# Identity products issued on TensorE ahead of its waits, in the attention block and the decay block of a four-layer network

## The reference

```
h = layernorm(x); q, k, v = h@wq+bq, h@wk+bk, h@wv+bv          # 64 wide
x = x + softmax(mask(q k^T / 8)) v @ wo + bo                   # causal, one head
h = layernorm(x); e = argmax(h@Wg + bg)                        # 1 of 8 experts
x = x + gelu(h@W1[e] + b1[e]) @ W2[e] + b2[e]
```

```
h = rmsnorm(x); mix tokens by decaying low-rank factors (h@u, h@v, length one)
and by a causal convolution of 4 taps, on h@proj_w; residual
h = rmsnorm(.); x = . + gelu(h@mlp_w1 + b1) @ mlp_w2 + b2
h = layernorm(x); x = x + gated linear map of the chosen expert (8 experts, capacity)
```

## Time and profile before

| what | value |
|---|---|
| median of 3 runs | 1574.55 us (1572.63 to 1575.88) |
| the profiled execution: its own time | 1564.02 us |
| its span from first to last instruction | 1562.3 us |
| mean granted TensorE clock | 0.891 |
| attention block (`c_`) in the trace | 1057.8 to 1324.8 us |
| decay block (`d_`) in the trace | 1324.8 us to the end |

### The profile page before, as it was taken

One profiled execution on the slowest core, in us unless ns is written; L12 is line 12 of the kernel. 1 busy time (PEld: TensorE's weight loads), 2 busy tenths in 40 slices (PEclk: granted clock), 3 DMA queues, 4 the chain that ended last, 5 costly groups with the idle time before them and its releaser, 6 DMA issues. The chain is left out here.

```text
span 1562.3 us, 21889 instructions
## 1 busy us (share of the span) xinstructions
PE 1274.7 (82%) x6731; PEld 720.4 (46%) x6731; DVE 1028.1 (66%) x2781; ACT 799.4 (51%) x1600; POOL 534.6 (34%) x668
## 2 busy tenths in 40 slices
PE   5899999999997128945589989985799997699898
PEld 1233333333332117941345655563476665477633
DVE  7878888888863665634897776323466654567486
ACT  2467777776774004526656653322445553466554
POOL 3442343343110005438555334431112112433046
PEclk7799999999999557975689999996799999699999
DMA  5211111111104402210023234221113131100001
GB/s 150 59 51 31 50 48 42 42 52 53 32 12 134 95 1 57 63 38 21 14 55 56 63 73 79 61 55 36 61 59 115 59 113 55 34 1 1 1 21 34
DMA packets 80775, 81.17 MB, mean 52 GB/s; under 512 B 19899, under 2 KB 64139, under 8 KB 80659
## 3 DMA queue, kind: packets, MB, share of 16 engines
q1 hardware_dynamic: 77327, 74.06, 18.2%
q0 software_dynamic: 2304, 4.72, 1.3%
q10 hardware_dynamic: 1028, 0.98, 0.2%
HBM read 64.32 MB, written 13.92 MB: 50 GB/s over the span
## 5 line engine op out<-in xcount | busy, mean ns | idle before, releaser
L933 DVE TENSOR_REDUCE a_nm<-a_aps 128x1 f32<-128x512 f32 x512 | 333.7, 687 | 74.7 <-PE a_aps L698 74.7
L897 ACT ACTIVATE a_prob<-a_sps 128x512 f32<-128x512 f32 x512 | 271.3, 597 | 114.6 <-PE a_sps L710 113.7
L698 PE MATMUL a_aps<-a_K,a_Q 96*128 96x512 bf16 x512 | 195.4, 402 | 12.5 <-DMA a_K<-k_parts 12.3
L710 PE MATMUL a_sps<-a_Q,a_K 99*128 99x512 bf16 x512 | 156.6, 386 | 1.2 <-ACT a_prob L897 1.2
L1402 POOL TENSOR_TENSOR p_h<-p_sl,p_t 128x512 f32<-128x512 f32 x72 | 105.5, 1483 | 144.6 <-issue 54.5
L719 PE MATMUL a_ops<-a_prob,a_Vg 128*32 128x512 f32 x1024 | 136.9, 609 | 0.0
L698 PEld LDWEIGHTS a_aps<-a_K,a_Q 96*128 96x128 bf16 x512 | 50.4, 98 | 139.9 <-DVE a_nm L933 89.8
L1542 ACT ACTIVATE p_sl<-p_up_a 128x512 f32<-128x512 f32 x72 | 42.9, 597 | 111.0 <-PE p_up_b L1432 111.0
L1934 POOL TENSOR_TENSOR c_h<-c_h,c_G 128x512 f32<-128x512 f32 x24 | 32.3, 1350 | 176.4 <-DMA c_G<-choice_rows 130.3
L407 POOL CAST a_ms<-a_mr 16x128 bf16<-16x128 f32 x32 | 9.0, 281 | 242.8 <-ACT a_mr L855 242.8
L1432 PE MATMUL p_up_b<-x_normT,p1w_w 128*128 128x512 f32 x144 | 75.9, 610 | 7.1 <-DVE p_t L1650 7.0
(11 more groups left out here) (574 smaller groups left out, 2687.8 us busy)
## 6 DMA issues: line engine op xcount, KB each, us to landing
p_G<-gates_by_expert SPq DMA_DIRECT2D x32, 512.0 KB, 7.7
c_G<-choice_rows SPq DMA_DIRECT2D x32, 512.0 KB, 6.4
a_Q<-q_parts SPq DMA_DIRECT2D x192, 32.0 KB
a_K<-k_parts SPq DMA_DIRECT2D x31, 96.0 KB
q_parts<-a_partsq SPq DMA_DIRECT2D x7, 384.0 KB, 2.8
k_parts<-a_partsk SPq DMA_DIRECT2D x7, 384.0 KB, 2.8
token_outputs<-m0e_y SPq DMA_DIRECT2D x40, 64.0 KB, 1.5
m0w_w<-in_L_ffn_W SPq DMA_DIRECT2D x1, 2048.0 KB, 8.6
```

Of the source, the lines that this page charges most:

```text
L698: nc.tensor.matmul(aps[n % 3][:, :], Q[0:MAX, head, q * P:(q + 1) * P], K[0:MAX, head, :], start=True, stop=True).then_inc(a_ready, 1)
L710: nc.tensor.matmul(sps[(NS * u + k) % 3][:, :], K[0:KB, head, k % TC * P:(k % TC + 1) * P], Q[0:KB, head, :], start=True, stop=True).then_ ...
L897: nc.scalar.activation(prob[u % 2][:, k // TC, k % TC, :], sps[n % 3][:, :], ACT.Exp).then_inc(p_done, 1)
L933: nc.vector.tensor_reduce(nm[u % 2][:, s:s + 1], aps[n % 3][:, :], AX.X, ALU.max, negate=True).then_inc(a_used, 1)
```

## The change

A helper `keep_busy` issues `n` products of the identity with itself into a PSUM bank. They have no waits and raise no semaphore, and nothing reads what they write. It is called at eight places of the attention block's TensorE program, all in steps -2 and -1 or ahead of them (97 products), and at five of the decay block's, in steps -2 to 0 or ahead of them (92 products; the call with 4 runs in two steps). Each call stands directly in front of an instruction group that waits. No wait and no other instruction is changed.

```diff
+def keep_busy(nc, net, bank, n):
+
+    for _ in range(n):
+        nc.tensor.matmul(bank, net.ident[:, :], net.ident[:, :], start=True, stop=True)
...
+            keep_busy(nc, net, hps[1][:, 0:P], 18)
             for s in steps:
                 if s + 1 == 0:
+                    keep_busy(nc, net, hps[1][:, 0:P], 9)
                     pe.wait_ge(bc_done, 1)
                 if here(s + 1):
                     weigh(s + 1)
...
                     if s + 2 == 0:
+                        keep_busy(nc, net, hps[1][:, 0:P], 4)
                         pe.wait_ge(qk_loaded, 64)
                     queries_and_keys(s + 2)
                     if s + 2 == 0:
                         join_tables()
+                        keep_busy(nc, net, hps[1][:, 0:P], 16)
                         scores(s + 2)
                     values(s + 2)
...
+                if s + 1 == 0:
+                    keep_busy(nc, net, hps[1][:, 0:P], 18)
                 if here(s + 1):
                     turn_second(s + 1)
...
                     if s + 1 == 0:
+                        keep_busy(nc, net, hps[1][:, 0:P], 4)
                         pe.wait_ge(g_loaded, 32)
                     logits(s + 1)
...
+                if s < 0:
+                    keep_busy(nc, net, hps[1][:, 0:P], 14)
                 if here(s + 2):
                     turn_prob(s + 2)
...
+            keep_busy(nc, net, yps[:, 0, :], 22)
             for s in steps:
+                if s <= 0 and here(s + 1):
+                    keep_busy(nc, net, yps[:, 0, :], 45 if s < 0 else 8)
                 if here(s + 1):
                     turn_factors(s + 1)
                 if here(s + 2):
                     turn_first(s + 2)
+                if s == 0:
+                    keep_busy(nc, net, yps[:, 0, :], 9)
                 if here(s):
                     turn_second(s)
...
                 if here(s + 2):
+                    if s < 0:
+                        keep_busy(nc, net, yps[:, 0, :], 4)
                     if s + 2 == 0:
                         pe.wait_ge(wide_scaled, 1)
                     project_wide(s + 2)
```

## The result

| kernel | median us | runs | lowest to highest |
|---|---|---|---|
| before | 1575.88 | 9 | 1572.63 to 1582.66 |
| changed | 1563.82 | 9 | 1551.12 to 1566.72 |

The ratio is 0.9911, with a 95% interval of 0.989 to 0.9932: the change takes 10.7 to 17.3 us off, 14.0 in the middle. (The ratios and intervals of this document are those on record; they need not equal the quotient of the two medians, which differ by 12.1 us here.) 1562 was forecast for the changed kernel and 12.7 us for the gain.

What follows compares the result with a forecast made beforehand. TensorE work at half clock (46.7 us) on the path of the attention and decay blocks' first steps was taken as the bound. Gains of 11.0 and 1.7 us gave 1574.55 - 12.7, about 1562 us; range 1555 to 1572.

Steps and rivals of the forecast that it cites:

- Prices: TensorE: an identity product takes 0.44 us at the lower clock and 0.224 us at the upper.
- Attention block, -11: Attention block up to step 0: faster groups less filling overshoots bring step 0's start 11 us earlier.
- the first rival: Saved time runs into another wait (VectorE, ScalarE or keys' DMA): half of the saving lost, 1568 us; chance 0.16.
- Every wait of the loop is relative, so these 11 us stay.: Attention block from step 0 on: the loop already ran at the upper clock, so the 11 us gain is kept.
- Decay block, -1.7: Decay block's first steps: overshoots of the opening fill and the 45, less faster groups, net 1.7 us gained.
- And the later steps keep it: Decay block's later steps: the 1.7 us gain is kept.
- Sum: Both blocks: -11.0 and -1.7 make -12.7 us, profiled 1564.02 to 1551.3, timed 1574.55 to about 1562.
- Identity products don't raise the clock: Third rival, all fillings: all 189 products run at 0.44 us, +46 us; slower outcomes had chance 0.10.
- The second rival: The clock falls at other places, varying by run: only 3 us gained, 1571.5 us; chance 0.12.

Runs made afterwards that it cites:

- e3: The changed kernel without the two opening fills (18 and 22 products behind the barriers): 1550.69 us against 1565.04 before, ratio 0.9899.
- e1: The changed kernel with only the attention block's 97 filling products, the decay block's removed: 1555.73 us against 1565.04 before, ratio 0.9937.
- e4: The changed kernel with every filling product streaming 8 identity columns in place of 128: 1599.22 us against 1565.04 before, ratio 1.0192.
- e5: The changed kernel with the decay block's filling of 45 products cut to 32: 1549.99 us against 1564.75 before, ratio 0.9909.
- c1: The changed kernel run a third time, unaltered, in another call: 1557.28 us against 1577.32 before, ratio 0.9887.
- e6: The changed kernel with more fillings, such as at the memory and attention blocks' ends, and refitted sizes: 1546.55 us against 1564.75 before, ratio 0.989.
- e7: As e6, but with the two opening fills left out: 1547.94 us against 1564.75 before, ratio 0.9892.
- c2: The kernel of e6 run again, unaltered, in another call: 1554.16 us against 1577.32 before, ratio 0.9869.
- e9: As e6, with the remaining gaps filled too (18 for 14, and 8 and 6 more products): 1551.73 us against 1577.32 before, ratio 0.9853.
- c0: The changed kernel run again, unaltered, in another call: 1552.61 us against 1564.75 before, ratio 0.9933.
- e2: The changed kernel with only the decay block's 92 filling products, the attention block's removed: 1564.18 us against 1565.04 before, ratio 0.9987.
- e8: The changed kernel with each filling product replaced by two 128x128 identity transposes: 1560.07 us against 1577.32 before, ratio 0.9901.

## Why the prediction was right, point by point

**Prices.** A filling product of 0.224 us at the upper clock: 32 instructions took 3.77 us (1079.80 to 1083.57), 0.236 a product. 90 took 10.04, 0.223. At the lower one, 8 instructions took 1.71 in e3 (1062.22 to 1063.93), 0.43 a product. Right.

**Attention block, -11.** Step by step against the barrier, forecast and measured: transposes +2.4, +2.5. Scores +1.2 (13.4 us behind the barrier), measured 1083.57 - 1069.99 = 13.6, +1.4. `turn_prob(0)` -1.9, measured 21.5 against 22.95, -1.5. Weighing -2.9, measured 24.6 against 27.2, -2.6. `turn_second(0)` -4.8, measured 34.0 against 38.7, -4.7. Step 0: -11, measured -11.1. The path was the one followed, and the first rival (half of the saving lost to another wait) falls. One premise was wrong without harm to the sum: the keys were to come at +1.0, 13.2 us behind the barrier, by a DMA as slow as before's. They came at 11.4, and the scores began at +1.4 because the filling of 16, sized for the slow DMA, ended then. The sum holds since it follows the filling's length; with a shorter one the saving could have been larger.

**"Every wait of the loop is relative, so these 11 us stay."** This step was wrong by 2.7 us in the changed kernel's trace. A0 is shorter by 11.1, the whole block by 8.4. The cause is in these rows, ahead of the last chunk's output products; the third is the like group before:

```profile
1314.58 0.77 PE L2055 MATMUL c_yps<-c_b,c_ohT 128*128 128x128 f32 x2 [3.37 <-issue]
1315.14 3.62 PE L2057 MATMUL c_yps<-c_W,c_h 128*128 128x128 f32 x16
...
1313.72 1.95 PE L2051 MATMUL c_yps<-c_W,c_h 128*128 128x128 f32 x16
```

A gap of 3.37 us, which stood there before as well (3.51), and then 16 instructions in 3.4 us. In the trace before the like group took 1.8. All four groups up to the block's end took 10.7 us here and 8.1 before, nearly all of the 2.7. The same loss, in part or whole, is in six of the eight traces that have attention fillings and none at this place (changed, e1, e3, e4, e5, c1), and in neither of the two traces without attention fillings; where the gap is filled (e6, e7, c2, e9) the groups were fast in all four. So the forecast overlooked that the clock can be lost later in a gap that didn't cost it before. Why it happens more often in the changed kernels stays open. e1 and c0 have 10.4 and 10.8 us of the gain left at the block's end.

**Decay block, -1.7.** The mechanism was right, and the sum held where its first premise did. The opening fill was put at +2.5, for a clock that is down when the block begins. It was +0.4 here and in c1, where the clock was still up, and +2.1 in c0 and e2, where it was down. I had taken its fall from a single trace. The delay was to reach VectorE's factors, less what the faster transposes give back (0.5), and where there was a delay it did: this is c0's row, barrier at 1315.45.

```profile
1332.22 0.79 DVE L2922 TENSOR_TENSOR d_K<-d_qn,d_tab 128x320 f32<-128x320 f32 x1
```

It ends 17.56 us behind the barrier, against 16.00 before: +1.6 (in e2 17.57, in the changed kernel's trace 15.94, with 5.03 - 4.60 = 0.4 of delay less 0.5). The overshoot of the 45 was 1.7 in both traces; 1.6 was forecast. So D2 was -1.9 in c0 and e2, close to the -1.7, and -3.6 in the changed kernel's trace, by the clock that was still up. "And the later steps keep it" was wrong for that trace: only 1.1 us are left at the end of the span. About 1 us went in the loop, and the rest at the first turned gates:

```profile
1487.54 0.39 PE L2663 MATMUL d_tps<-ident,d_gates 128*32 128x128 f32 x1 [2.19 <-DVE d_gates L3028]
1487.72 1.96 PE L2684 MATMUL d_kps<-d_WT,x_normT 128*128 128x512 f32 x2
1489.48 1.66 PE L2684 MATMUL d_qps<-d_WT,x_normT 128*128 128x512 f32 x2
```

The gap of 2.19 is one of before's (2.20), and the products behind it took 1.76 and 1.59 us from start to start where before they took 0.91 and 0.96: 1.5 us lost. Of the ten traces without a filling there three have this loss (changed, c1, e2) and seven don't, and none of the four with a filling (e6, e7, c2, e9) has it.

**Sum.** -12.7 forecast; -14.0 measured (10.7 to 17.3), with -10.5 (c0) and -17.8 (c1) in other calls. How closely it held is partly luck: in the traces the two blocks together are shorter by 9.5 us (changed), 12.9 (c0) and 12.2 (c1), where the ratios give 14.0, 10.5 and 17.8. So up to 6 us of a ratio lie outside the two blocks, and the stages ahead move by as much between executions. For the profiled execution itself 1551.3 was given and 1566.72 came. Of the 15.4 between them 12.2 are of the stages ahead, which this change doesn't touch, and 3.2 are missing in the two blocks, which gained 9.5 for the 12.7.

**Rivals.** "Identity products don't raise the clock" is refuted: they ran at 0.22 to 0.24 us. Its price was of the right kind, though: e4 shows what a filling costs that doesn't raise it (+30 by the ratio, +15.9 in A0 and +17 in D2). The second rival, the clock falling elsewhere, is real but small: it took 2.7 and 1.5 us in one trace.

## What to carry to other kernels

Where a pipeline fills and TensorE alternates with one other engine, half the clock is paid on the path itself, and filling products win it back; their number is the wait ahead of the group divided by the product's time at the upper clock, measured to the moment when the other engine or the DMA is ready, since each product too many delays the real one by its full length. Look for that moment again in the trace with the fillings: a group that follows directly on a filling may have been kept by it, as the scores were for 2.1 us. Fill the idle stretch ahead of a barrier too, and not the one behind it alone (e6). Small gaps in a sparse stretch, like those of 1.0, 1.8 and 3.4 us here, lost the clock in some executions and not in others; filling them is worth a trial. Compare such variants by block lengths and by medians of many runs: which gaps lose the clock differs between executions of one kernel.

## What the runs showed of the hardware that was not expected

- A stretch in which TensorE is shown busy without a gap can stay at the lower clock: products with 8 streamed columns left it at 0.43 us a product (e4), while those with 128 columns and pairs of 128-column transposes took 0.22 to 0.24.
- Transposes of the identity raised the clock and held it (0.114 us each, e8).
- The DMA that moves the keys took 4.0 us to land in the two traces without attention fillings, issued 8.1 us behind the barrier, and 2.2 or 2.3 in the twelve with them, issued after 6.7 to 12.2 us. In the two slow cases one part of it landed 1.7 us behind all the others. The cause stays open.
- One kernel's opening fill of 18 products ended 5.76, 5.77 and 4.13 us behind its barrier in three executions, that of 22 5.03, 6.66 and 5.02; the Trainium skill, "TensorE: Matmul & The Clock Gate", Part 1, says that the count of slow products at a start varies from run to run, and the rows agree.
- The kernel before had medians of 1575.88, 1565.04, 1564.75 and 1577.32 in the four calls, so its level moved by 0.8% from call to call, as much as the change is worth; the three calls of the experiments ran on three different chips. In the traces the difference lies ahead of the attention block: its barrier came at 1055.1 to 1059.2 us in the calls with 1565, and at 1063.5 to 1067.5 in the one with 1577, while an earlier barrier, at 488 to 491 us, hardly differs. What makes it is left unexplained; the ratios are taken within a call.
